# Attention steps with the expert's totals behind the Gram products, the high half of W1 last, and the expert tables made once

## The reference

```python
x = x + _layernorm(attn(_layernorm(x), Wq, bq, Wk, bk, Wv, bv, gamma))
x = x + _layernorm(ffn(_layernorm(x), W1, b1, W2, b2, gate_W, shared_W, shared_b, lng, lnb))
# attn: Q, K, V = x @ W.T + b; Q and K normed over the rows;
#   (V.sum + Q.T (K V.T)) / (L + Q . K.sum + eps), then x + gamma * that
# ffn: top 2 of softmax(x @ gate_W); out = 0.5 * gelu(x @ shared_W + shared_b)
#   + sum over the two of weight * (gelu(x @ W1[e] + b1[e]) @ W2[e] + b2[e]); layer norm
```

## Time and profile before

| | |
|---|---|
| median of the three runs | 691.05 us |
| the profiled execution: its own time | 688.41 us |
| the profiled execution: span from first to last instruction | 686.6 us |
| mean granted TensorE clock | 0.960 of full speed |
| PE busy | 590.0 us (86%) |
| VectorE (DVE) busy | 465.6 us (68%) |
| ScalarE (ACT) busy | 444.1 us (65%) |
| GpSimd (POOL) busy | 321.1 us (47%) |

### The profile page before, as it was taken

The page is one execution under the profiler, slowest core; times in us unless marked ns, Lnnn a source line. Parts: engine busy times, 40 slices in busy tenths (PEclk is TensorE's granted clock), DMA queues, the critical chain, the costliest instruction groups (busy, mean ns, idle before and its releaser), DMA issues.

```text
span 686.6 us, 16884 instructions
## 1 busy us (share of the span) xinstructions
PE 590.0 (86%) x4903; PEld 510.2 (74%) x4903; DVE 465.6 (68%) x1242; ACT 444.1 (65%) x875; POOL 321.1 (47%) x511
## 2 busy tenths in 40 slices
PE   4768988988887799999998999999999999999400
PEld 3657776777765588989897787989898998988300
DVE  5469999999987664544677676544444445778884
ACT  2647577677755584757555878757575665877653
POOL 4000234533626833578757332334343455664694
PEclk9989999999999999999999999999999999999855
DMA  7645564562155332113114221221211259641566
GB/s 250 213 149 188 184 185 125 185 220 86 66 170 202 105 128 79 48 34 95 33 47 126 79 63 49 75 82 48 79 56 48 56 106 226 118 94 61 115 163 122
DMA packets 45273, 78.25 MB, mean 114 GB/s; under 512 B 16963, under 2 KB 30597, under 8 KB 44805
## 3 DMA queue, kind: packets, MB, share of 16 engines
q1 hardware_dynamic: 33492, 48.19, 21.6%
q0 software_dynamic: 11696, 28.98, 17.6%
HBM read 48.17 MB, written 28.98 MB: 112 GB/s over the span
## 4 chain that ended last, share of the span: by engine, by line
PE 50%; DVE 29%; issue 8%; ACT 7%; POOL 3%; DVEq 1%; DMA 1%; ACTq 1%; POOLq 0%
PE banks L537 13%; PE banks L538 13%; PE banks L539 13%; ACT X L1531 3%; DVE st L1618 3%; PE banks L1209 2%; DVE W L1764 2%; DVE W L1768 2%; PE banks L1107 2%; ACT W L1391 1%; DVE zone L1707 1%; PE banks L1039 1%; DVE stage L1997 1%; PE banks L974 1%; ACT stage L1537 1%
## 5 line engine op out<-in xcount | busy, mean ns | idle before, releaser
L1531 ACT ACTIVATE X<-banks,b1T,tab 128x256 f32<-128x256 f32 x256 | 129.0, 553 | 101.2 <-PE banks L539 79.6
L1997 DVE SCALAR_TENSOR_TENSOR stage<-X,tab,stage 128x512 f16<-128x512 f32 (+1 forms) x160 | 109.3, 697 | 118.5 <-ACT stage L1537 112.7
L537 PE MATMUL banks<-W,stage 128*128 x576 | 157.1, 273 | 3.8 <-DVE stage L1997 2.4
L538 PE MATMUL banks<-W,stage 128*128 x576 | 157.0, 273 | 0.0
L539 PE MATMUL banks<-W,stage 128*128 x576 | 157.0, 273 | 0.0
L537 PE MATMUL banks<-X,W 128*128 128x256 f16 x512 | 140.3, 274 | 5.0 <-DVE X L2011 3.9
L538 PE MATMUL banks<-X,W 128*128 128x256 f16 x512 | 140.3, 274 | 0.0
L539 PE MATMUL banks<-X,W 128*128 128x256 f16 x512 | 140.2, 274 | 0.0
L839 POOL DMA_INDIRECT y_rows<-X,tb x72 | 81.4, 1131 | 102.4 <-DVE X L2028 77.8
L1537 ACT ACTIVATE stage<-X,tab 128x512 f16<-128x512 f32 (+1 forms) x160 | 106.9, 677 | 10.7 <-ACT X L1531 6.9
L826 POOL DMA_INDIRECT X<-xf_rows,tb x72 | 75.0, 1041 | 55.1 <-issue 34.2
(11 more groups left out here) (301 smaller groups left out, 1147.7 us busy)
## 6 DMA issues: line engine op xcount, KB each, us to landing
stage<-in_L_ffn_W SPq DMA_DIRECT2D x10, 1024.0 KB, 10.5
W<-in_L_ffn_W SPq DMA_DIRECT2D x6, 1024.0 KB, 7.3
X<-in_L_attn_x SPq DMA_DIRECT2D x8, 512.0 KB, 5.0
out<-X SPq DMA_DIRECT2D x8, 512.0 KB, 3.4
xf_rows<-zone SPq DMA_DIRECT2D x8, 512.0 KB, 4.1
u_rows<-b2b SPq DMA_DIRECT2D x8, 512.0 KB
X<-y_rows POOLq DMA_DIRECT2D x8, 512.0 KB, 8.1
away<-W SPq DMA_DIRECT2D x1, 2048.0 KB, 7.5
```

Of the source, the lines that this page charges most:

```text
L537: pe.matmul(o, lh, rh, start=first, stop=False)
L538: pe.matmul(o, lh, rl, start=False, stop=False)
L1531: a.activation(tile, tile if joint(j) else PS[m][:, r * BT:(r + 1) * BT], ACT.Gelu, bias=b1T[:, bass.ds(e * NH + 2 * m + r, 1)], scale=tab ...
L1997: v.scalar_tensor_tensor(o[1], src, tab[:, 1, bass.ds(e, 1)], o[0], ALU.mult, ALU.subtract).then_inc(h_low, 1)
```

## The change

On every engine the change moves calls inside `step`, and it takes instructions out of the expert's part.

- TensorE: `totals` comes behind `grams` of the entering batch, no longer ahead of it.
- ScalarE: `xf_high` follows `cosines_out` directly; then `totals_out`, `gram_out`, `expert_scales`, `xfT_out` and only then `w2_highs`. `w1_highs` moves from ahead of the first `shared_out` to between the second and the third.
- VectorE: `expert_bounds` moves from behind `inverses` to behind `xf_low`; the cut to powers of two (`expert_powers`) stands behind `mix_out`; `w1_lows` moves from ahead of `mixT_out` to behind `enter_stats`.
- `expert_bounds` has three instructions, not four (a factor 2 goes into the square of b1). `expert_tables` has one left in each step. The other work is done once for all experts in `all_tables`, three instructions in the last step. ScalarE waits for them ahead of its first Gelu.

```diff
@@ TensorE, step
                     cosines(mixing)
+                if entering is not None:
+                    grams(entering)
                 if i is not None:
                     totals(i)
-                if entering is not None:
-                    grams(entering)
@@ ScalarE, step
                     q_roots(mixing)
-                if i is not None:
-                    totals_out(i)
                 if leaving is not None:
                     spread(2, x1_dev, (x1_mean, T * (leaving + 1)), 0, 1.0 / SX / SX)
                 if mixing is not None:
                     cosines_out(mixing)
+                if leaving is not None:
+                    xf_high(leaving)
+                if i is not None:
+                    totals_out(i)
+                if entering is not None:
+                    gram_out(entering)
                 if i is not None:
                     expert_scales(i)
                 if leaving is not None:
-                    xf_high(leaving)
-                if entering is not None:
-                    gram_out(entering)
+                    xfT_out(leaving)
                 if i is not None:
                     w2_highs(i)
-                if leaving is not None:
-                    xfT_out(leaving)
-                if i is not None:
-                    w1_highs(i)
                 if leaving is not None:
                     shared_out(leaving, 0)
                 if mixing is not None:
                     mix_scale(mixing)
                 if leaving is not None:
                     shared_out(leaving, 1)
+                if i is not None:
+                    w1_highs(i)
+                if leaving is not None:
                     shared_out(leaving, 2)
@@ VectorE
-                link(v.scalar_tensor_tensor(ebnd[:, 2:3], etot[:, 0:1], float(D), etot[:, 2:3], ALU.mult, ALU.add))
-                link(v.tensor_scalar(ebnd[:, 0:2], etot[:, 0:2], 1e-24, None, ALU.max))
-                link(v.tensor_scalar(ebnd[:, 2:3], ebnd[:, 2:3], 2.0, 1e-24, ALU.mult, ALU.max))
+                link(v.scalar_tensor_tensor(etot[:, 2:3], etot[:, 0:1], 2.0 * D, etot[:, 2:3], ALU.mult, ALU.add))
+                link(v.tensor_scalar(ebnd[:, 0:3], etot, 1e-24, None, ALU.max))
                 link(v.reciprocal(ebnd[:, 0:3], ebnd[:, 0:3]))
-            def expert_tables(i):
+            def expert_powers(i):
                 v.wait_ge(expert_roots, i + 1)
-                link(v.tensor_scalar(escl[:, 0:3].bitcast(I32), escl[:, 0:3].bitcast(I32), EXP_MASK, None, ALU.bitwise_and))
-                link(v.tensor_scalar(einv[:, 0:3].bitcast(I32), escl[:, 0:3].bitcast(I32), -1.0, EXP_FLIP, ALU.mult, ALU.add))
-                link(v.tensor_scalar(tab[:, 0, e:e + 1], einv[:, 0:1], 1.0 / SX, None, ALU.mult))
-                link(v.tensor_copy(tab[:, 1, e:e + 1], escl[:, 2:3]))
-                link(v.tensor_tensor(tab[:, 2, e:e + 1], einv[:, 1:2], einv[:, 2:3], ALU.mult))
+                link(v.tensor_scalar(escl[:, :, e].bitcast(I32), escl[:, :, e].bitcast(I32), EXP_MASK, None, ALU.bitwise_and))
+            def all_tables():
+                link(v.tensor_scalar(einv[:, :, :].bitcast(I32), escl[:, :, :].bitcast(I32), -1.0, EXP_FLIP, ALU.mult, ALU.add))
+                link(v.tensor_scalar(gelu_scale[:, :], einv[:, 0, :], 1.0 / SX, None, ALU.mult))
+                link(v.tensor_tensor(down_scale[:, :], einv[:, 1, :], einv[:, 2, :], ALU.mult))
@@ VectorE, step
                     inverses(mixing)
-                if i is not None:
-                    expert_bounds(i)
                 if leaving is not None:
                     leave(leaving)
-                if i is not None:
-                    expert_tables(i)
                 if mixing is not None:
                     tailor_factors(mixing)
                 if leaving is not None:
                     xf_low(leaving)
+                if i is not None:
+                    expert_bounds(i)
                 if mixing is not None:
                     mix_out(mixing)
+                if i is not None:
+                    expert_powers(i)
+                if mixing is not None:
                     tailor(mixing)
                 if leaving is not None:
                     xfT_out(leaving)
                 if i is not None:
                     w2_lows(i)
-                    w1_lows(i)
                 if mixing is not None:
                     mixT_out(mixing)
...
                 if after is not None:
                     enter_stats(after)
+                if i is not None:
+                    w1_lows(i)
                 if leaving is not None:
                     pick_experts(leaving)
```

More of the change, by code:

```diff
@@ L24 @@
 LOW_ROW = 32
-EV_BOUNDS, EV = 4, 9
+EV_BOUNDS, EV = 3, 4
+TABLES = 3
 EXP_MASK = 0x7F800000
@@ L125, in sandwich @@
         ebnd = sb("ebnd", [P, 4], F32)
-        escl = sb("escl", [P, 4], F32)
-        einv = sb("einv", [P, 4], F32)
-        tab = sb("tab", [P, 3, E], F32)
+        escl = sb("escl", [P, 3, E], F32)
+        einv = sb("einv", [P, 3, E], F32)
+        gelu_scale = sb("gelu_scale", [P, E], F32)
+        down_scale = sb("down_scale", [P, E], F32)
+        high_scale = escl[:, 2, :]
         slot_i = sb("slot_i", [P, B, 2, T], I32)[:, :, :, :]
@@ L1398, in expert_scales @@
                 settle(a)
-                a.activation(escl[:, 0:3], ebnd[:, 0:3], ACT.Sqrt, scale=TOP * TOP).then_inc(expert_roots, 1)
+                e = TURN[i]
+                a.activation(escl[:, :, e], ebnd[:, 0:3], ACT.Sqrt, scale=TOP * TOP).then_inc(expert_roots, 1)
             def w1_highs(i):
@@ L1404, in w1_highs @@
                 settle(a)
-                a.activation(w1_part(slot(i), 0), staged(i, 0), ACT.Copy, scale=escl[:, 0:1]).then_inc(w1_high, 1)
+                a.activation(w1_part(slot(i), 0), staged(i, 0), ACT.Copy, scale=escl[:, 0, TURN[i]:TURN[i] + 1]).then_inc(w1_high, 1)
             def w2_highs(i):
@@ L1410, in w2_highs @@
                 settle(a)
-                a.activation(w2_part(slot(i), 0), staged(i, 1), ACT.Copy, scale=escl[:, 1:2]).then_inc(w2_high, 1)
+                a.activation(w2_part(slot(i), 0), staged(i, 1), ACT.Copy, scale=escl[:, 1, TURN[i]:TURN[i] + 1]).then_inc(w2_high, 1)
             def step(s):
@@ L1537, in gelu @@
                         a.activation(hhl[:, j % 2, 2 * m:2 * m + 2, 0, span(j, p)], h32[:, m % 2, :].rearrange("p (r n) -> p r n", r=2)[:, :, span(j, p)],
-                                     ACT.Copy, scale=tab[:, 1, bass.ds(e, 1)]).then_inc(h_high, 1)
+                                     ACT.Copy, scale=high_scale[:, bass.ds(e, 1)]).then_inc(h_high, 1)
             def lean_of(j):
@@ L1569, in _ @@
             a.wait_ge(blocks_ready, 1)
+            a.wait_ge(expert_steps, EV * E + TABLES)
             gelu(0, 0, 2)
@@ L1754, in expert_tables @@
                 v.wait_ge(expert_roots, i + 1)
-                link(v.tensor_scalar(escl[:, 0:3].bitcast(I32), escl[:, 0:3].bitcast(I32), EXP_MASK, None, ALU.bitwise_and))
-                link(v.tensor_scalar(einv[:, 0:3].bitcast(I32), escl[:, 0:3].bitcast(I32), -1.0, EXP_FLIP, ALU.mult, ALU.add))
-                link(v.tensor_scalar(tab[:, 0, e:e + 1], einv[:, 0:1], 1.0 / SX, None, ALU.mult))
-                link(v.tensor_copy(tab[:, 1, e:e + 1], escl[:, 2:3]))
-                link(v.tensor_tensor(tab[:, 2, e:e + 1], einv[:, 1:2], einv[:, 2:3], ALU.mult))
-                assert link.count[0] == EV - EV_BOUNDS
+                link(v.tensor_scalar(escl[:, :, e].bitcast(I32), escl[:, :, e].bitcast(I32), EXP_MASK, None, ALU.bitwise_and))
+                assert link.count[0] == EV - EV_BOUNDS
+            def all_tables():
+                link = chain(v, expert_steps, EV * E)
+                link(v.tensor_scalar(einv[:, :, :].bitcast(I32), escl[:, :, :].bitcast(I32), -1.0, EXP_FLIP, ALU.mult, ALU.add))
+                link(v.tensor_scalar(gelu_scale[:, :], einv[:, 0, :], 1.0 / SX, None, ALU.mult))
+                link(v.tensor_tensor(down_scale[:, :], einv[:, 1, :], einv[:, 2, :], ALU.mult))
+                assert link.count[0] == TABLES
             def w1_lows(i):
                 v.wait_ge(w1_high, i + 1)
-                v.scalar_tensor_tensor(w1_part(slot(i), 1), staged(i, 0), escl[:, 0:1], w1_part(slot(i), 0), ALU.mult, ALU.subtract).then_inc(w1_low, 1)
+                v.scalar_tensor_tensor(w1_part(slot(i), 1), staged(i, 0), escl[:, 0, TURN[i]:TURN[i] + 1], w1_part(slot(i), 0), ALU.mult, ALU.subtract).then_inc(w1_low, 1)
             def w2_lows(i):
                 v.wait_ge(w2_high, i + 1)
-                v.scalar_tensor_tensor(w2_part(slot(i), 1), staged(i, 1), escl[:, 1:2], w2_part(slot(i), 0), ALU.mult, ALU.subtract).then_inc(w2_low, 1)
+                v.scalar_tensor_tensor(w2_part(slot(i), 1), staged(i, 1), escl[:, 1, TURN[i]:TURN[i] + 1], w2_part(slot(i), 0), ALU.mult, ALU.subtract).then_inc(w2_low, 1)
             def block_of(count):
@@ L1939, in last_step @@
                 expert_bounds(E - 1)
```

(7 more changed lines are left out.)

6 lines of the change are left out of this document (3 added, 3 removed).

## The result

The changed kernel takes 698.45 us (median of 4 runs, 695.06 to 699.95), where the kernel before takes 691.21 beside it (4 runs). The ratio is 1.0100, with a 95% interval of 1.0059 to 1.0141. The forecast was 695.5 within 690.0 to 699.0. A second measurement (the experiment `e9_changed_again`) gave 697.51 against 689.82, a ratio of 1.0107 (1.0070 to 1.0143). So the difference is 7.2 to 7.7 us, where 4.45 were forecast.

A forecast was written before the change was run, and what follows sets the result against it. A step was taken as VectorE's instructions plus its waits. Five steps at 0.93 (4.65), plus 1.1 for step 6, minus 1.3 for step 0, gave 4.45 us on the median 691.05: 695.5, range 690.0 to 699.0.

The forecast's parts named there:

- The signs: Trace after: steps 25.3 to 25.7 us, VectorE busy about 22.2, three new waits, `w2_highs` about 2 us later, `attend` not released by `mixT_out`.
- The walk: VectorE's changed step 5, laid out start by start from rows of the old trace; it made a step 0.94 us longer.
- +0.93: Lengthening per step: minus 0.98 for instructions, minus 0.38 for old waits, plus 0.39, 0.84 and 1.02 for new waits.
- the 0.17 that `pick_experts` was to win back: VectorE's old wait ahead of L1731, for a copy; it was to vanish because `pick_experts` comes later than that copy.
- The third wait: VectorE ahead of `w2_lows`, waiting for ScalarE's `w2_highs`, now behind the bounds: 1.02 us a step, the largest new wait.
- the halfway rival: W2's high half is ready in time, so no wait ahead of `w2_lows`: steps 0.1 us shorter, 689.2 us, chance 0.09.
- The price of moving `w1_lows`: VectorE's `w2_lows`, `w1_lows`, `mixT_out` and `enter_stats` keep their sum of 6.73 us in another order.
- Step 0: No leaving batch; `mixT_out` comes earlier, so `attend` starts earlier: 1.3 us less, bounded by 0.5 and 1.6.
- The clock: Rival: longer TensorE idle time ahead of `shared` lowers its clock in each of six steps: 707 us, chance 0.04.
- The last expert's W1: Rival: its load, issued later behind `w1_lows(6)`, lands late for the last step's squares: up to 698.0 us, chance 0.07.
- the full gain: Rival: VectorE is saturated and no new waits appear, 1.36 us a step saved: 681.6 us, chance 0.04.
- no difference: Rival: the waits come out about 0.7 us a step smaller: 691 us within 1.4, chance 0.09.

The follow-up runs named there:

- e9_changed_again: The changed kernel measured again with no edit: 697.51 us against 689.82 for the kernel before, ratio 1.0107.
- e1_tables_once: Kernel before, call order kept, with three bounds instructions, one for powers per step and the tables made once: 691.56 us against 690.73, ratio 1.0015.
- e6_w2_unscaled: Changed kernel with W2's high half made without its scale, ahead of `expert_scales` (output not the reference's): 695.89 us against 690.13 for the kernel before.
- e2_w1_last: Kernel before with only W1's halves moved: high behind the second `shared_out`, low behind `enter_stats`. 695.96 us against 690.73, ratio 1.0077.
- e4: Changed kernel with unread filler matmuls from step 1 on, 12 ahead of `key_norms` and 20 ahead of `shared`: 694.87 us, ratio 1.0070 to kernel before.
- e10: Changed kernel with 12 unread filler matmuls ahead of `key_norms` only: 700.61 us, ratio 1.0156 to the kernel before.
- e11: Changed kernel with 20 unread filler matmuls ahead of `shared` only: 696.88 us, ratio 1.0091 to the kernel before.
- e12_both_undone: Changed kernel with W1's halves in their old places and W2's high half unscaled, ahead of the roots: 718.21 us on another chip, ratio 0.9876 to kernel before.

## Why the prediction was right, and where not

**The direction and the mechanism** held. The sum of the saved instructions is worth nothing by itself (`e1_tables_once`), and VectorE's waits of 0.44, 0.67 to 0.88 and 1.02 to 1.17 us stand where 0.39, 0.84 and 1.02 were forecast.

The signs came in part. `w2_highs` starts 11.23 us into step 3, for 9.10 before, and in steps 1 to 6 `attend` follows a wait of 1.25 us for the third `shared_out`, as forecast. VectorE was to be busy for 22.2 us and is for 22.76. Of the six steps one lies in the 25.3 to 25.7 that were given.

**The walk** through the step can be laid over step 3 of after, start by start, in us from `products`. It gave `leave` at 5.33, `xf_low` at 8.21, `mix_out` at 9.99 and `w2_lows` at 13.19. The trace has 5.34, 8.23, 9.97 and 13.25. Durations and semaphores of one trace were enough for that.

**The step is +1.1 to +1.4, not +0.93.** The term that was wrong is the 0.17 that `pick_experts` was to win back. It was read in step 5, the one step of before that has that wait. Step 3 of before, by its timeline, does not have it:

```profile
120.59 0.19 DVE L1730 TENSOR_REDUCE zone<-b2b 128x4 f32<-128x32 f32 x1
120.81 0.19 DVE L1731 TENSOR_TENSOR zone<-b2b,zone 128x32 f32<-128x32 f32 x1
```

Without it the sum is 1.10, and step 3 has 1.08, step 6 1.20 (forecast 1.1). Step 4 has 0.15 more ahead of `w2_lows` and 0.17 in `enter` (L1643, 1.53 us for 1.36). Step 1 has 0.2 more ahead of the statistics of `attended`. The mean of these four is 1.26, and six times that is 7.6, not 5.75: 1.8 us of the miss.

**The third wait was right in size and wrong as a cause.** "`mixT` is there at 167.0 [...] so moving `mixT_out` forward brings nothing in these steps" took for granted that `turn_mix` would be ready. It is ready only then: `mixT_out`, released by it, starts 15.46 us into the step of `e6_w2_unscaled`. That `mixT_out` came out in time was luck: the wait ahead of `w2_lows` had used up exactly what the second path needs. For the same reason the halfway rival ("the third wait alone is absent", 689.2) was no real case. `e6_w2_unscaled` is that case, and its steps did not become shorter. The price of moving `w1_lows` was put at nothing ("keep their sum in another order"); alone it costs 5.2 us (`e2_w1_last`, the gain of step 0 already taken off), since it uncovers the wait for `turn_mix`.

**Step 0** gained 3.4 us, not 1.3, and what the gain exceeds the forecast by is the clock's. From the start of `cosines` to that of `mixT_out` it is 13.06 us (28.28 to 41.34) for 14.47 (28.89 to 43.36), 1.41 less, where 1.36 were forecast: the walk held here too. The other 0.6 by which `attend` starts earlier lie ahead of `cosines`, at a granted clock of 0.91 from 26 to 28 us for 0.59 before. And `attend` itself took 1.3 us less. The prediction kept the durations of stretches in which the clock was still coming back. That this helped was luck of the profiled execution: step 0 has the same code in `e4`, `e9`, `e10` and `e11`, the 13.06 come again in each within 0.01, and `attend` takes 4.38, 5.82, 6.35 and 6.26 us, the step 23.32, 24.28, 25.85 and 25.58.

**The clock** was a rival with a chance of 0.04, priced for every step (707). It came in part. Two of six steps of the profile had a stretch at 0.54, at 0.7 to 0.8 us each above the mean of the others, 1.5 us in all. In the last step, priced at 0, `attend` took 1.6 us longer at a clock of 0.69 for 1.00. The Trainium skill describes in "TensorE: Matmul & The Clock Gate", section "HAM oscillation", a loop that falls back to the low clock on every pass. Here the trace agrees only for single passes, not for every one. Against the forecast of 4.45, then: +1.8 for the steps, +1.5 for the clock in them, +1.6 in the last step, -2.1 in step 0 and -0.6 in the experts' part. That is 6.65, of 6.7 measured in the profiled executions. So the clock cost 3.1 us in steps 2 and 5 and the last step and gave 1.9 back in step 0.

**The range.** By its own bounds the forecast reaches from 693.7 to 697.8 (six times 0.7 less 1.6, and six times 1.2 less 0.5), not from 693.3 to 697.5. The measured 698.45 lies above either. It lies inside 690.0 to 699.0 only because that range was made wider for the rivals, and a second measurement of the same kernel has single runs up to 702.57.

**The last expert's W1** was not late. The last step's squares of W1 (L1394, 208.39) come 2.6 us behind its `products`, and before 3.2 us. The other rivals, the full gain and no difference, did not come.

## What to carry to other kernels

Before small instructions are taken away from a full engine or moved on it, look at what comes ready while they run: here they stood in front of a 1.06 us wait, and taking 0.98 us away gained nothing until others were moved into the gap. Where a wait is to be removed, walk the other inputs of the next instructions too, since a second path may be as long. Read a small wait in several passes of a loop before it goes into a sum.

## What the runs showed of the hardware

The granted clock can fall in single passes of a loop of which the other passes keep the full clock, and another execution of the same kernel has it in other passes: steps 2 and 5 in the first profile, 1, 2 and 5 in the second. The kernel before shows it in none of steps 1 to 6. Beside it stands a wide spread: the changed kernel took 693.23 to 702.57 us in six runs, where the kernel before stayed within 687.66 to 692.02 in eleven beside it.

The same 16 matmuls of step 0 took 4.36 to 6.35 us in five executions with the same code up to there, by how soon the granted clock was back at 1.00.

One of the chips ran the kernel before 5% slower than the others (725.61 us). The one profile taken on it (`e12_both_undone`) has VectorE's instructions at their usual durations (2.34 us for the low half of W2), and 24.5 of its 26.5 us more than `e6_w2_unscaled` lie behind the experts' first product. A copy of VectorE there (L2019) waits 23.0 us in all, which the profile puts down to none of this core's engines, and in `e6_w2_unscaled` it has no such wait. What it waits for is not known.
